# Small loads on spaced partitions in the last two passes, and the final pass without a loop

## The chip, the cores and the metric

The kernel runs on one core of a Trainium2 chip. The metric is the device time of one execution in microseconds (us). The times before are 3980.14, 3980.3 and 4032.01 us, the median 3980.3.

## The reference, cut to what matters

The input x has 16 images of 64 channels and 256 x 256 points, in float32. Two residual layers follow each other.

```
# layer 0
g   = groupnorm(x, groups=32)
F   = rfft2(g)[..., :32, :17]                       # 32 x 17 modes are kept
Y   = einsum('bhixy,hioxy->bhoxy', F, weight)       # 4 heads of 16 channels
x1  = x + irfft2(Y, padded with zeros) + bias
# layer 1, on g1 = groupnorm(x1, groups=32), all points of all images
m     = mean(g1);  mu = m / sqrt(m0^2 - |m1..|^2)   # Lorentz mean
alpha = max(g1_0 mu_0 - g1_rest . mu_rest, 1 + eps) # one value a point
d     = arccosh(alpha);  var = mean(d^2)            # over everything
v     = d / sqrt(alpha^2 - 1) * (g1 - alpha mu)
vo    = v - v_0 / (1 + mu_0) * (mu + e_0)
s     = gamma * vo_rest / (sqrt(var) + eps) + beta
out   = x1 + concat(sqrt(1 + |s|^2), s)             # channel 0, channels 1..63
```

## The kernel before, in words

Three passes read x. The first (`stage_a`) computes the kept modes and the norms' sums and writes the mixed modes to `spec`. It is not touched, apart from being followed by the others.

The middle pass (`stage_b`, from line 559) computes alpha and its relatives for every point of an image. x comes in eight tiles of 2 MB an image (`b_xt`, SyncE's queue, four buffers) and TensorE contracts the channels of each tile (L663). For the part of x1 that comes from the modes, GpSimd loads the image's modes into `b_spt` (`load_modes`, L753; 64 partitions, two loads of 32 rows each), VectorE contracts the channels in `combine` (products L818 and L824 with `arow` and `lrow`, sums L821 and L825, on 64 partitions x 2176 elements), and TensorE transforms the result (L673 to L685) and adds it to the contraction of x. `dense` (L839 to L868) then makes, from the finished image, the factor rows, splits each in three bf16 parts, and GpSimd stores them as `maps` (L773), `bmap` (L774) and `dmap` (L775), and only then takes up the next image: its weights (L747) and its `load_modes`. VectorE's order in a turn is combine of an image, then dense of the one before. GpSimd's order is weights, modes of the image, three words a channel into `spec` (L760), channel 0 of x (L767, after dense has read the last one), and the stores.

The final pass (`stage_c`, from line 967) writes the output. An image is 16 tiles of 128 partitions x 2048 (1 MB): partition p holds half a channel. Per tile TensorE makes the modes' part (L1118, from `c_mv`, whose last two rows of each half are loaded from bmap) and VectorE adds it to x (L1262); TensorE makes a factor and a shift (L1132, from `c_rt`: twelve rows, six to each half, as bf16, times a weight matrix `lwc` that is zero on all rows but those), VectorE multiplies (L1272), ScalarE copies the shift (L1198) and squares (L1205), GpSimd adds (L1323), TensorE sums the squares for channel 0 (L1143). Channel 0 is finished once an image and stored by itself (L1057, four stores of 32 rows).

SyncE issues every transfer of this pass, in a written order: per tile the small loads of the tile after next (per half three of `c_rt` with 6, 4 and 2 rows, L1032, and one of `c_mv`, L1033, so eight), the x load of that tile (L1022), the store of the tile two back (L1039). Once an image come channel 0's stores (L1057), two halves of modes for the next image (L1043) and `c_dmap` (L1049). The weights' rows of `c_rt` are marked in the constant `misc` (columns 12 to 23), which `place` (in the middle pass) turns into `keep["lw"]`. Images 1 to 14 are a hardware loop on each engine; as an operand can't be indexed by image in it, ScalarE copies that image's weights and two columns to `lwc` and `cols` (L1214, L1221) at its end.

Of the kernel before, what the change touches and what calls it, by code (L numbers as in the profile page):

```python
# [20 lines left out]
ALU = mybir.AluOpType  # L21
# [12 lines left out]
EPS = 1e-5  # L34


def constants():
# [521 lines left out]
def stage_b(nc, ctx, io, B, keep):  # L559
# [19 lines left out]
    NC_IN = 16 * 16  # L579

    with ExitStack() as mem:
# [13 lines left out]
        arow, lrow = sb("arow", [128, B, C]), sb("lrow", [128, B, C])  # L595
        aw, awc = sb("aw", [128, B, 2, 2]), sb("awc", [128, 2, 47])
# [4 lines left out]
        spt = sb("spt", [64, C, YS])  # L601
        prod = sb("prod", [64, C, M2])
# [15 lines left out]
        def _(sp):  # L618
# [16 lines left out]
            sp.dma_start(idft_h[0:64], cst["idft_d"]).then_inc(c_in, 16)  # L635
# [105 lines left out]
        def _(pool):  # L741
# [66 lines left out]
        def _(dve):  # L808
# [5 lines left out]
            def combine(b):  # L814

                dve.wait_ge(sp_in, b * 32 + 32)
# [5 lines left out]
                V.tensor_copy(vm[0:64, 1], spt[:, 0, 0:M2]).then_inc(v_ready, 1)  # L822
                dve.wait_ge(v_ready, b * 3 + 2)
                ch.step(V.tensor_tensor(prod[:], spt[:, :, 0:M2], over_m(lrow[0:64, b]), ALU.mult))  # L824
                V.tensor_reduce(vm[0:64, 2], prod[:].rearrange("p c m -> p m c"), AX_X, ALU.add).then_inc(v_ready, 1)  # L825
# [67 lines left out]
            ch.inc(V.memset(vm[:], 0.0))  # L893
            V.memset(idft_h[64:128], 0.0).then_inc(setup, 1)
# [72 lines left out]
def stage_c(nc, ctx, io, B, keep):  # L967
# [23 lines left out]
    with ExitStack() as mem:  # L991
# [23 lines left out]
        def _(sp):  # L1015
# [35 lines left out]
            def store_channel_0(b):  # L1051
# [4 lines left out]
                for j in range(4):  # L1056
                    sp.dma_start(o0_v[b, 0, j], o0[32 * j:32 * j + 32]).then_inc(o0_out, 16)  # L1057
# [342 lines left out]
```

## Time and profile before

| | |
|---|---|
| Runs, us | 3980.14, 3980.3, 4032.01 |
| Profiled execution, us | 4024.94, of which its span is 4023.4 |
| Granted TensorE clock, mean | 0.878 of full |
| Busy: PE, DVE, ACT, POOL | 75%, 68%, 53%, 38% |
| Transfers | 1199.08 MB, 298 GB/s over the span |
| SyncE's queue | 266126 packets, 1152.07 MB, 79.9% of 16 engines |

The profile is of one execution; a row's time is from the span's start. The first pass ends near 1130 us, the middle one near 2060 us, and the final one runs to the end. "Share" of the transfers is the mean busy share of the sixteen transfer engines (DMA engines). "To landing" is the time from a transfer's issue to its last completion. A queue's instructions carry the suffix q (SPq is SyncE's, POOLq GpSimd's).

### The profile page before, as it was taken

Reading aid. Unit: us, or ns where it says so; the run is one execution under the profiler, and the core shown is the slowest. Engines: PE = TensorE matmul, PEld = TensorE weight load, DVE = VectorE, ACT = ScalarE, POOL = GpSimd, SP = SyncE. Lnnn points to the kernel's source line nnn. Section 1 sums busy time; section 2 is a strip of 40 time slices with the busy share of each in tenths; the row PEclk is TensorE's granted clock in tenths of the full one; section 3 lists DMA queues with packets and bytes.
Section 4 is the critical chain, followed back from the end, with each engine's and each line's share of the span. In section 5 each row is a group of like instructions: output and inputs, shape, how many; then the busy total and the mean of one; then the engine's idle time right before and its main releaser. Section 6 shows DMA issues by size and latency. Waiting matters only on the chain. (4 is left out here: it accounts for less than half of the span.)

```text
span 4023.4 us, 77883 instructions
## 1 busy us (share of the span) xinstructions
PE 3002.5 (75%) x26018; PEld 1495.1 (37%) x26018; DVE 2748.0 (68%) x2969; ACT 2141.8 (53%) x2940; POOL 1513.6 (38%) x876
## 2 busy tenths in 40 slices
PE   6988898989446767677715877877777778877776
PEld 3555555555211222222203434344333344443332
DVE  1888888888865355555444767677777677777766
ACT  6777676767200011111014767677776677776665
POOL 0110101010111111111113766666666666666666
PEclk9988888988668888888857999999999999999999
DMA  9878777677269999999915989899999899999898
GB/s 373 287 256 282 260 265 274 244 285 253 76 259 354 325 341 376 362 361 374 334 53 183 337 313 329 313 325 321 313 315 320 306 330 334 329 334 311 311 314 288
DMA packets 280512, 1199.08 MB, mean 298 GB/s; under 512 B 35145, under 2 KB 37038, under 8 KB 197934
## 3 DMA queue, kind: packets, MB, share of 16 engines
q1 hardware_dynamic: 266126, 1152.07, 79.9%
q0 software_dynamic: 14112, 43.37, 3.4%
q8 instruction: 171, 2.80, 0.3%
q14 instruction: 103, 0.84, 0.1%
HBM read 883.53 MB, written 311.73 MB: 297 GB/s over the span
## 5 line engine op out<-in xcount | busy, mean ns | idle before, releaser
L1323 POOL TENSOR_TENSOR c_ot<-c_ot,c_pp 128x1024 f32<-128x1024 f32 x512 | 1211.8, 2368 | 727.0 <-DVE c_ot L1272 651.8
L1262 DVE SCALAR_TENSOR_TENSOR c_xt<-c_xt,keep_k,c_p_u 128x1024 f32<-128x1024 f32 x512 | 654.0, 1277 | 332.5 <-DMA c_xt<-in_x 170.8
L1118 PE MATMUL c_p_u<-c_mv,c_zc 64*128 64x256 f32 x4096 | 612.3, 420 | 225.1 <-DVE c_xt L1262 163.1
L1272 DVE SCALAR_TENSOR_TENSOR c_ot<-c_p_f,keep_k,c_xt 128x1024 f32<-128x1024 f32 x512 | 657.3, 1284 | 177.0 <-DMA out<-c_ot 134.4
L1198 ACT ACTIVATE c_pp<-c_p_p,c_cols 128x1024 f32<-128x1024 f32 x512 | 570.5, 1114 | 362.4 <-PE c_p_p L1132 359.0
L1205 ACT ACTIVATE c_sq<-c_xt,c_cols 128x1024 f32<-128x1024 f32 x512 | 584.2, 1141 | 139.5 <-DVE c_xt L1262 138.8
L1118 PEld LDWEIGHTS c_p_u<-c_mv,c_zc 64*128 64x128 f32 x4096 | 371.4, 195 | 532.9 <-DVE c_xt L1262 321.3
L327 ACT ACTIVATE a_junk<-a_xt 128x1024 bf16<-128x1024 f32 x512 | 537.2, 1053 | 28.8 <-DMA a_xt<-in_x 21.5
L246 PE MATMUL a_p_rows<-a_xt,a_dft_h 128*64 128x512 f32 x2048 | 517.5, 652 | 33.6 <-DMA a_bias_t<-in_bias 19.5
L1132 PE MATMUL c_p_f<-c_rt,c_lwc 64*128 64x512 bf16 x1024 | 328.0, 402 | 179.6 <-DVE c_ot L1272 161.3
L663 PE MATMUL b_p_al<-b_xt,b_awc 128*32 128x512 f32 x2048 | 312.4, 682 | 161.2 <-DMA b_xt<-in_x 116.3
L721 ACT ACTIVATE b_dn<-b_dn,b_minus 128x512 f32<-128x512 f32 x16 | 11.6, 722 | 730.4 <-DVE b_dn L842 730.4
L525 POOL TENSOR_TENSOR a_sm<-a_sm 128x8 f32<-128x8 f32 x16 | 26.7, 1670 | 931.0 <-DVE a_sm L460 931.0
L1132 PE MATMUL c_p_p<-c_rt,c_lwc 64*128 64x512 bf16 x1024 | 330.7, 405 | 0.0
L399 DVE TENSOR_REDUCE a_y<-a_prod 128x34 f32<-128x1088 f32 x256 | 317.4, 1281 | 5.7
L394 DVE TENSOR_TENSOR a_prod<-a_wm,a_xh 128x1088 f32<-128x1088 f32 x256 | 318.0, 1284 | 0.3
L818 DVE TENSOR_TENSOR b_prod<-b_spt,b_arow 64x2176 f32<-64x2176 f32 x16 | 38.7, 2417 | 393.3 <-DMA b_spt<-spec 393.3
L1143 PE MATMUL c_p_t<-c_sq,c_hw 128*32 128x512 f32 x2048 | 305.1, 671 | 1.2 <-ACT c_sq L1205 1.2
L663 PE MATMUL b_p_ls<-b_xt,b_awc 128*32 128x512 f32 x2048 | 297.3, 650 | 0.0
L1104 PEld LDWEIGHTS c_p_z<-c_idft,c_ys 128*37 128x37 f32 x7936 | 238.0, 116 | 111.3 <-issue 111.3
L1104 PE MATMUL c_p_z<-c_idft,c_ys 128*37 128x64 f32 x7936 | 277.3, 224 | 0.0
L271 PE MATMUL a_p_cols<-a_dft_w,a_cols 128*128 128x34 f32 x2048 | 264.5, 288 | 3.1 <-DVE a_xm L388 3.1
(209 smaller groups left out, 3029.8 us busy)
## 6 DMA issues: line engine op xcount, KB each, us to landing
a_xt<-in_x SPq DMA_DIRECT2D x256, 1024.0 KB, 8.0
b_xt<-in_x SPq DMA_DIRECT2D x128, 2048.0 KB, 16.0
c_xt<-in_x SPq DMA_DIRECT2D x256, 1024.0 KB, 16.7
out<-c_ot SPq DMA_DIRECT2D x256, 1024.0 KB, 18.4
maps<-b_maps POOLq DMA_DIRECT2D x64, 192.0 KB, 5.7
dmap<-b_dmap POOLq DMA_DIRECT2D x16, 768.0 KB, 11.6
c_rt<-maps SPq DMA_DIRECT2D x512, 24.0 KB
c_dmap<-dmap SPq DMA_DIRECT2D x16, 768.0 KB, 17.2
```

The lines of the kernel that those rows point to most:

```text
L246: last = nc.tensor.matmul(p_rows[i][64 * t:64 * t + 64, :], dft_h[:, j], xt[q % NX][:, t::2, i, j * W:(j + 1) * W], start=(j == 0), stop=( ...
L327: nc.scalar.activation(junk[h % 2][:].rearrange("p (i w) -> p i w", i=2), xt[q % NX][:, h], ACT.Square, accum_out=sq[:, q, h:h + 1]).then_ ...
L394: ch.inc(V.tensor_tensor(prod[o % 2][:], wm[:, o], xh[:].rearrange("p k n -> p (k n)").unsqueeze(1).to_broadcast((128, 2, CI * M2)), ALU.m ...
L663: last = nc.tensor.matmul(out[32 * j:32 * j + 32, :], awc[:, kind, 15 - k:47 - k], xt[t % NX][:, at:at + 512], start=(k == 0), stop=False, ...
L1104: last = nc.tensor.matmul(p_z[64 * at:64 * at + YS, 64 * c:64 * c + 64], ys[:, 8 * part + c], idft[:, chunk, at], start=True, stop=True)
L1118: last = nc.tensor.matmul(p_u[:, 512 * at + W * r:512 * at + W * r + W], zc[t // CH][64 * at:64 * at + 64, i], mv[t % NB][64 * at:64 * at ...
L1132: last = nc.tensor.matmul(p[:, 512 * k:512 * k + 512], lwc[at:at + 64], rt[t % NB][at:at + 64, c:c + 512], start=True, stop=True)
L1198: S.activation(pp[n][:], p_p[:], ACT.Identity, bias=cols[:, 1:2]).then_inc(pp_done, 1)
L1205: S.activation(sq[t % 2][:, 1024 * n:1024 * n + 1024], xt[t % NB][:, 1024 * n:1024 * n + 1024], ACT.Square, scale=cols[:, 0:1]).then_inc(s ...
L1262: V.scalar_tensor_tensor(out=u, in0=u, scalar=kc, in1=p_u[:], op0=ALU.mult, op1=ALU.add).then_inc(u_done, 1)
L1272: V.scalar_tensor_tensor(out=ot[t % NB][:, at], in0=p_f[:], scalar=kinv, in1=xt[t % NB][:, at], op0=ALU.add, op1=ALU.mult).then_inc(f_done, 1)
L1323: P.tensor_tensor(o, o, pp[n][:], ALU.add).then_inc(o_done, 1)
```

## The change

The loads of `c_rt` put their twelve rows at partitions 5, 15, ... 115, 14, 30, ... 126 and 16, 48, 80, 112 instead of 0 to 11 and 64 to 75, and both halves come with one load each: three loads a tile instead of six. The mask columns follow. The `c_ys` modes go to every second partition, with the constant `c_idft` beside them. Channel 0's four stores become one. In the middle pass `b_spt` holds two heads on each half of the partitions, so combine runs on 128 partitions x 1088 elements, with copies `ah` and `lh` of the factors; its load becomes four of 64 rows. The final pass is written out for all sixteen images, without the loop and without `lwc`, `cols` and `idle`.

```diff
+MAP_ROWS = ((5, 10), (14, 16), (16, 32))
...
-    for at, first in ((12, 0), (18, 64)):
-        for part, (row, rows) in enumerate(((0, 6), (6, 4), (10, 2))):
-            for s in range(2):
-                m[first + row + s:first + row + rows:2, at + 2 * part + s] = 1.0
+    for a, at in enumerate((12, 18)):
+        for part, ((first, step), rows) in enumerate(zip(MAP_ROWS, (6, 4, 2))):
+            for i in range(rows):
+                m[first + step * (rows * a + i), at + 2 * part + i % 2] = 1.0
...
-                for k in range(2):
-                    pool.dma_start(spt[KX * k:KX * k + KX].rearrange("k (h i) m -> k h (i m)", h=HEADS),
-                                   spec[b, k].rearrange("(h k) n -> k h n", h=HEADS)).then_inc(sp_in, 16)
+                for h in range(HEADS):
+                    half, i = 64 * (h // 2), 16 * (h % 2)
+                    pool.dma_start(spt[half:half + 64, i:i + 16].rearrange("p i m -> p (i m)"),
+                                   spec[b, :, KX * h:KX * h + KX]).then_inc(sp_in, 16)
...
-                over_m = lambda a: a.unsqueeze(2).to_broadcast((64, C, M2))
-                ch.step(V.tensor_tensor(prod[:], spt[:, :, 0:M2], over_m(arow[0:64, b]), ALU.mult))
+                over_m = lambda a: a.unsqueeze(2).to_broadcast((128, C // 2, M2))
+                ch.step(V.tensor_tensor(prod[:], spt[:, :, 0:M2], over_m(ah[:, b]), ALU.mult))
...
-                V.tensor_reduce(vm[0:64, 0], prod[:].rearrange("p c m -> p m c"), AX_X, ALU.add).then_inc(v_ready, 1)
+                V.tensor_reduce(vm[:, 0], prod[:].rearrange("p c m -> p m c"), AX_X, ALU.add).then_inc(v_ready, 1)
...
+            for half in range(2):
+                p, c = slice(64 * half, 64 * half + 64), slice(32 * half, 32 * half + 32)
+                ch.inc(V.tensor_copy(ah[p], arow[p, :, c]))
+                ch.inc(V.tensor_copy(lh[p], lrow[p, :, c]))
...
-    maps_v = io["maps"].rearrange("b m s (t n) -> b t (m s) n", n=TC)
+    maps_v = io["maps"].rearrange("b (a m) s (t n) -> b t a (m s) n", a=2, n=TC)
...
+                for (first, step), rows in zip(MAP_ROWS, (6, 4, 2)):
+                    sp.dma_start(r[first:first + step * (2 * rows - 1) + 1:step], maps_v[b, t, :, :rows]).then_inc(r_in[t % NB], 16)
                 for at in range(2):
-                    for row, rows in ((0, 6), (6, 4), (10, 2)):
-                        sp.dma_start(r[64 * at + row:64 * at + row + rows], maps_v[b, t, 6 * at:6 * at + rows]).then_inc(r_in[t % NB], 16)
                     sp.dma_start(m[64 * at + M2:64 * at + M2 + 2].rearrange("p (n r) -> p n r", n=2), bmap_v[b, t, at]).then_inc(r_in[t % NB], 16)
...
-                    sp.dma_start(ys[KX * k:KX * k + KX, 32 * half:32 * half + 32].rearrange("k (h i) m -> k h (i m)", h=2),
+                    sp.dma_start(ys[64 * k:64 * k + 64:2, 32 * half:32 * half + 32].rearrange("k (h i) m -> k h (i m)", h=2),
...
-                for j in range(4):
-                    sp.dma_start(o0_v[b, 0, j], o0[32 * j:32 * j + 32]).then_inc(o0_out, 16)
+                sp.dma_start(o0_v[b, 0], o0[:]).then_inc(o0_out, 16)
...
-            entry(0)
-            with sp.Fori(1, B - 1) as b:
-                entry(b)
-            entry(B - 1, last=True)
+            for b in range(B):
+                entry(b, last=b == B - 1)
...
-                S.activation(pp[n][:], p_p[:], ACT.Identity, bias=cols[:, 1:2]).then_inc(pp_done, 1)
+                S.activation(pp[n][:], p_p[:], ACT.Identity, bias=keep["cols"][:, b, 1:2]).then_inc(pp_done, 1)
```

The same replacement of the loop stands on the other four engines, and L1132 reads `keep["lw"]` of its image instead of `lwc`.

## Rows read from the trace of the kernel before

**Rows 1.** Windows, middle and final pass: us; busy (count) by engine; clock; DMA share; GB/s.
```profile
1260.00:1980.00 720.00, 499.94 (x3498) 165.00 (x3490) 357.60 (x325) 78.22 (x117) 116.70 (x218) 0.84 0.94 350
2205.20:3949.50 1744.30, 1364.00 (x15402) 690.54 (x15404) 1279.05 (x1022) 1230.18 (x1293) 1157.45 (x497) 0.94 0.92 321
```

**Rows 2.** The line L1049 (once an image): duration in ns min/median/max, first and last start.
```profile
L1049 SPq DMA_DIRECT2D c_dmap<-dmap x16: 332/392/970, 2205.2 to 3949.5; - x16
```

**Rows 3.** SyncE's order of time, first tiles of the final pass: start us, us, instruction.
```profile
2188.27 0.37 SPq L1039 DMA_DIRECT2D out<-c_ot  x1
...
2199.29 0.37 SPq L1039 DMA_DIRECT2D out<-c_ot  x1
```

**Rows 4.** Transfers from 2100 to 2129 us, while c_mv's 37 constant rows load.
```profile
DMA packets 637, 0.65 MB, mean 22 GB/s; under 512 B 5, under 2 KB 637, under 8 KB 637
...
q1 hardware_dynamic: 637, 0.65, 6.7%
```

**Rows 5.** SyncE's order of time at the loop's back edge in the final pass.
```profile
3074.60 0.38 SPq L1039 DMA_DIRECT2D out<-c_ot  x1
3081.72 1.05 SPq L1032 DMA_DIRECT2D c_rt<-maps  x3
```

**Rows 6.** Windows before and after that back edge reaches the transfers.
```profile
3076.00:3081.00 5.00, 4.07 (x56) 2.35 (x54) 3.90 (x4) 3.77 (x5) 3.50 (x3) 1.00 0.97 298
3082.40:3086.40 4.00, 1.37 (x8) 1.08 (x10) 0.61 (x1) 1.40 (x4) 2.83 (x2) 0.88 0.19 70
```

**Rows 7.** Transfers of one image, 3019.6 to 3139.3 us: GB/s in 40 slices, packets.
```profile
GB/s 264 331 414 372 426 349 379 297 382 282 311 375 407 231 256 348 374 374 168 259 360 68 211 315 368 305 412 374 295 258 339 312 315 329 320 391 128 242 287 285
DMA packets 6266, 37.44 MB, mean 313 GB/s; under 512 B 1108, under 2 KB 1108, under 8 KB 2132
```

**Rows 8.** Order of time in the middle pass: one turn, then the first and last loads.
```profile
1543.49 0.56 POOL L775 DMA_DIRECT2D dmap<-b_dmap  x1
1544.70 1.22 POOL L753 DMA_DIRECT2D b_spt<-spec  x2 [0.45 <-issue]
1561.16 2.42 DVE L818 TENSOR_TENSOR b_prod<-b_spt,b_arow 64x2176 f32<-64x2176 f32 x1 [25.46 <-DMA b_spt<-spec]
1563.62 4.22 DVE L821 TENSOR_REDUCE b_vm<-b_prod 64x34 f32<-64x2176 f32 x1
...
1575.28 0.75 DVE L839 TENSOR_SCALAR b_dn<-b_p_al,b_ac 128x512 f32<-128x512 f32 x1 [0.59 <-DVE b_vm L825]
...
1590.57 0.59 POOL L773 DMA_DIRECT2D maps<-b_maps  x1 [10.96 <-DVE b_maps L868]
...
1596.72 1.22 POOL L753 DMA_DIRECT2D b_spt<-spec  x2 [0.44 <-issue]
...
1252.65 1.20 POOL L753 DMA_DIRECT2D b_spt<-spec  x2 [0.16 <-issue]
...
1980.52 1.23 POOL L753 DMA_DIRECT2D b_spt<-spec  x2 [0.44 <-issue]
```

**Rows 9.** The page's transfers: out<-in, queue, count, KB each, median us to landing.
```profile
c_xt<-in_x SPq DMA_DIRECT2D x256, 1024.0 KB, 16.7
...
c_rt<-maps SPq DMA_DIRECT2D x512, 24.0 KB
c_dmap<-dmap SPq DMA_DIRECT2D x16, 768.0 KB, 17.2
b_spt<-spec POOLq DMA_DIRECT2D x32, 296.0 KB, 16.1
...
c_mv<-bmap SPq DMA_DIRECT2D x512, 8.0 KB
```

**Rows 10.** Groups by line, final pass: a table load of ScalarE at each turn's head.
```profile
L1198 ACT ACT_TABLE_LOAD x14 | 18.0, 1283 | 43.4 <-PE c_p_p L1132 43.3
```

**Rows 11.** The page's groups: VectorE on 128x1088, in the first pass.
```profile
L399 DVE TENSOR_REDUCE a_y<-a_prod 128x34 f32<-128x1088 f32 x256 | 317.4, 1281 | 5.7
L394 DVE TENSOR_TENSOR a_prod<-a_wm,a_xh 128x1088 f32<-128x1088 f32 x256 | 318.0, 1284 | 0.3
```

More of the change, by code:

```diff
@@ L634, in _ @@
             sp.dma_start(btrow[:], row(io["beta"], C)).then_inc(c_in, 16)
-            sp.dma_start(idft_h[0:64], cst["idft_d"]).then_inc(c_in, 16)
+            for half in range(2):
+                sp.dma_start(idft_h[64 * half:64 * half + 64], cst["idft_d"]).then_inc(c_in, 16)
             sp.dma_start(idft_w[:], cst["idft_w"]).then_inc(c_in, 16)
@@ L923, in _ @@
             ch.step(V.tensor_tensor(v1[:], over_b(brow[:]), srow[:, :, 1], ALU.subtract))
+            for half in range(2):
+                p, c = slice(64 * half, 64 * half + 64), slice(32 * half, 32 * half + 32)
+                ch.inc(V.tensor_copy(ah[p], arow[p, :, c]))
+                ch.inc(V.tensor_copy(lh[p], lrow[p, :, c]))
             ch.inc(V.tensor_scalar(q2[:], srow[:, :, 0, 0], s1(5), None, ALU.mult))
@@ L1001, in stage_c @@
         sq = [sb(f"sq{k}", [128, TC]) for k in range(2)]
-        lwc = sb("lwc", [128, 2 * C], BF16)
-        cols, idle = sb("cols", [128, 2]), sb("idle", [128, 1])
         dmap = sb("dmap", [128, 3, 512])
@@ L1123, in factors @@
                 g = b * GR + 2 * t + n
-                if t == 0 and n == 0:
-                    pe.wait_ge(w_ready, b + 1)
                 if not (is_at(b, 0) and t == 0 and n == 0):
@@ L1131, in factors @@
                         c = 1024 * n + 512 * k
-                        last = nc.tensor.matmul(p[:, 512 * k:512 * k + 512], lwc[at:at + 64], rt[t % NB][at:at + 64, c:c + 512], start=True, stop=True)
+                        last = nc.tensor.matmul(p[:, 512 * k:512 * k + 512], keep["lw"][at:at + 64, b].rearrange("p c s -> p (c s)"), rt[t % NB][at:at + 64, c:c + 512], start=True, stop=True)
                 last.then_inc(f_mm, 1)
@@ L1164, in _ @@
             pe.wait_ge(c_in, 16 * (2 + 2 * NB))
-            pe.wait_ge(filled, 3)
+            pe.wait_ge(filled, 2)
             for part in range(8):
@@ L1174, in _ @@
                 ins.then_inc(z_mm, 1)
-            entry(0)
-            with pe.Fori(1, B - 1) as b:
-                entry(b)
-            entry(B - 1, last=True)
+            for b in range(B):
+                entry(b, last=b == B - 1)
             sums(B - 1, T - 1)
@@ L1211, in root @@
                 S.activation(th[:], arg[:], ACT.Sqrt).then_inc(th_ready, 1)
-            def weights(b):
-                S.activation(lwc[:], keep["lw"][:, b].rearrange("p c s -> p (c s)"), ACT.Copy).then_inc(w_ready, 1)
-            def columns(b):
-                if not is_at(b, 0):
-                    act.wait_ge(pp_done, b * GR)
-                    act.wait_ge(sq_done, b * GR)
-                    S.activation(idle[:], idle[:], ACT.Copy).then_inc(cols_free, 1)
-                S.activation(cols[:], keep["cols"][:, b], ACT.Copy).then_inc(cols_ready, 1)
             def entry(b, last=False):
@@ L1229, in entry @@
                     shift(b, t, 1)
-                    if t == T - 1 and not last:
-                        weights(b + 1)
                     square(b, t, 1)
@@ L1234, in entry @@
                         root(b - 1)
-                if not last:
-                    columns(b + 1)
-            weights(0)
-            columns(0)
             act.wait_ge(zeroed, 2 * NB + 2)
-            act.wait_ge(filled, 3)
+            act.wait_ge(filled, 2)
             for part in range(8):
                 copy_part(0, part, part + 1)
-            entry(0)
-            with act.Fori(1, B - 1) as b:
-                entry(b)
-            entry(B - 1, last=True)
+            for b in range(B):
+                entry(b, last=b == B - 1)
             root(B - 1)
@@ L1298, in _ @@
             V.memset(ys[:], 0.0).then_inc(zeroed, 1)
-            V.memset(idft[64:128], 0.0).then_inc(filled, 1)
+            V.memset(idft[:], 0.0).then_inc(zeroed, 1)
             V.memset(p_z[:], 0.0).then_inc(filled, 1)
-            V.memset(idle[:], 0.0).then_inc(zeroed, 1)
             V.memset(hw[:], 0.0).then_inc(chain, 1)
@@ L1306, in _ @@
             ch.done = 1
-            entry(0)
-            with dve.Fori(1, B) as b:
-                ch.loop(b, 1, PER_C)
+            for b in range(B):
                 entry(b)
-                ch.end(B - 1)
             channel_0(B - 1)
@@ L1336, in entry @@
                         channel_0(b - 1)
-            entry(0)
-            with pool.Fori(1, B) as b:
+            for b in range(B):
                 entry(b)
             channel_0(B - 1)
-PER_C = 2
 def program(nc, args, B):
```

35 lines of the change are left out of this document (16 added, 19 removed).

## The prediction

> **What bounds the kernel now.** I read the page's slices and queues first, then the two later passes (from lines 559 and 967) in windows, then the packets of single stretches, then SyncE's and VectorE's order of time. The profiled execution took 4024.9 us, 1.1% over the median of the runs, 3980.3; all differences below are worked out against the profiled one and put on the median. The change leaves the first pass (to about 1130 us) alone.
>
> The final pass, from 2205 to 3950 us, has the transfer engines busy for 0.92 of the time at 321 GB/s, while no compute engine passes 0.8 [rows 1]. An image takes (3949.5 - 2205.2)/15 = 116.3 us, 7.27 us a tile [rows 2]. Compute alone can do 5.51 us: that is the step of the first tiles (11.02 us for two), before SyncE's queue has filled [rows 3]. So transfers set the pace. But which? Two rows show that it isn't all sixteen engines. A load onto 37 rows runs at 22 GB/s and 6.7% of the engines, one of sixteen [rows 4]: a load goes to as many engines as its rows divide into. And at the loop's back edge SyncE issues nothing for 6.7 us [rows 5]; the engine share then falls from 0.97 to 0.19 [rows 6], three engines' worth, with 70 GB/s still moving. Some engines hold a backlog that the others don't. Who they are follows from a count: in one image 1108 packets are under 512 B [rows 7], where no data row is that small; they are completions, one for each engine that took part. The 41 wide transfers of an image (32 of x and out, 4 of modes, 1 of dmap, 4 of channel 0) take 656. The other 452, 28 a tile, are the eight small loads: 2 x (6 + 4 + 2 + 2). Each small load therefore uses as many engines as its outermost count, and I take them to be the same first ones each time. Per tile the first two engines then carry 6 rows of 4 KB of c_rt and 8 KB of c_mv beside their 128 KB of x and out.
>
> A check: a busy engine moves 321/(0.92 x 16) = 21.8 GB/s. Per image the first two have 2.10 MB of x and out (33.5 MB over sixteen), 0.52 MB small and 0.10 MB of the rest (c_dmap, c_ys, channel 0; sizes in [rows 9]): 125 us at that rate, against 116 measured; the others have 101 us. The first two must run 7% better (23.4 GB/s) while others idle, which fits. They are the bound, and the rest has 13% slack.
>
> The middle pass is different: 56.0 us an image ((1980.5 - 1252.7)/13), in a closed circle that one turn shows [rows 8]: POOL issues b_spt at 1544.7; it lands at 1561.2; combine takes VectorE to 1575.0; dense and its casts last until POOL can store the maps at 1590.6; after the nine stores it issues the next b_spt at 1596.7: 52.0 us with no slack in it.
>
> **The change, part by part.**
>
> *Final pass, c_rt (L1032).* Six loads a tile become three, of 12, 8 and 4 rows; with c_mv five issues where there were eight. SyncE's issues of 0.3 us each [rows 5] are saved, 0.9 us a tile, hidden: its stretched issues are back pressure, it is ahead of the data (c_xt lands 16.7 us after its issue [rows 9]). The bytes stay. What counts is rows on the first two engines, now 6. Bounds: if each load's rows spread one to an engine, 3 rows, -3 x 0.175 us x 16 = -8.4 us an image (-134 us in all; 4096 B at 23.4 GB/s is 0.175 us); if all three went to two engines, 12 rows, +16.8 us (+269). The source of the 12 is evenly spaced (six of six rows), so it is one count of 12. The sources of the 8 and of the 4 are two separate groups, 2 x 4 and 2 x 2; the nearest row is c_mv, a 2 x 2 pattern of four pieces, which by the count above uses 2 engines, not 4. So I take 1 + 4 + 2 = 7 rows: +1 row, +2.8 us an image, 45 us in all.
> The Trainium skill ("DMA: Bandwidth & Descriptors", section "Why a DMA increments its semaphore by 16 and not by 1") says that the engine count is the largest up to 16 that divides the slowest dimension of both sides, and on SyncE's queue the lowest-numbered engines. It names 12, 2 and 2 engines for the new loads; the trace's 28 completions agree with it, and no row here shows a load whose two sides differ in this.
>
> *Channel 0's store (L1057).* Four stores of 32 rows become one whose outermost count is 4: by the same reading 32 rows of 2 KB on each of four engines instead of 8 on all: +49 KB on the first two, 2.1 us an image, 34 us in all. Bounds 0 (if it spreads) to 34.
>
> *Landing places.* The small rows now land from partition 5 to 126 instead of 0 to 11 and 64 to 75. What that relieves no row shows; from below nothing, from above the whole lag of the first two, 15 us an image. The check above closes without any crowding, so I take a value near the lower end, a tenth: 1.6 us an image, -25 us.
>
> *No loop.* The back edge costs SyncE some 6 us more than its usual gap [rows 5] and ScalarE a table load of 1.28 us at its head [rows 10]. I cost it at nothing: the two late engines work through it on their backlog (rows 6's 70 GB/s). If that cover were gone, it would be up to the 4 us lull a turn, 56 us. Copies of lwc and cols (ScalarE) go as well; ScalarE is not the bound.
>
> *Middle pass, combine (L818 to L825).* Two products of 64x2176 at 2.42 us and two sums at 4.22 us become 128x1088. The product of that size takes 1.28 us [rows 11]; a sum is half of 4.22, 2.1 (the contiguous one of the same size takes 1.28 [rows 11], this one is strided). 13.9 us become 7.3: -6.6 a turn, between -8.3 and -5.
>
> *Middle pass, load of the modes (L753).* Two loads of 32 rows become four of 64 rows, the source in two groups of 32. By the same reading each goes to 2 engines. Whether the four pairs differ no row shows; the ends are one pair for all and four pairs, and I take four, which is nearer to the even load that every transfer from this queue shows now: 76 KB on each of eight engines instead of 38 on all. Per engine dmap's 48 KB and b_spt's 38 KB land in 17.7 us (1543.5 to 1561.2), beside the x stream: 4.9 GB/s. So +38 KB are +7.7 us. Bounds: 0 if they still use sixteen; +54 us if all four went to the same two (303 KB each). Landing is in the circle, and POOL issues two more (0.6 us each) but behind dmap's packets: nothing. Net +1.1 us x 14 turns = +15 us. If the circle gets shorter, the x stream, at 350 GB/s now [rows 1], has room for it: slices of the final pass reach 426 [rows 7].
> The same page says that loads from GpSimd take their two engines in turn, by a cursor, which gives eight and +7.7 us; no run here shows it yet.
>
> *One-offs.* Four copies (ah, lh) and one more constant load ahead of the first turn, about 2 us; three store issues less at the very end, -1.
>
> Sum: +45 + 34 - 25 + 0 + 15 + 1 = +70 us: 4095 on the profiled execution, **4050** on the median (+1.8%).
>
> **Rivals.**
> 1. *Relief.* The small rows sat on the same few partitions that the first engines write x to; spread, both run freely. For it: the two late engines are just those. Against: the rate check closes without it. If half of the 15 us lag goes, -7.6 us x 16 = -122, and with the middle pass level 3860. The Trainium skill ("SBUF — State Buffer", "Door 1: The DMA port swizzle") holds that partitions 0 to 63 reach only half of the ports to the memory and four adjacent ones a single port; by that rule the time falls, by some part of this sum. No row here separates one port's load from another's.
> 2. *Only the middle pass gains.* b_spt still lands in 16 us: -6.6 x 14 = -92, the final pass +54: 3942.
> 3. *Slower.* The twelve rows go to two engines as well (their source is written as two halves): 12 rows instead of 7, +5 x 0.175 x 16 x 16 = +224 on the forecast: 4275. It decides as soon as the first load's completions are 2 instead of 12. The fixed pair in the middle pass would be worse still (+46 x 14 = +640 and more).
> 4. *It does nothing*: the 321 GB/s are the memory's own limit for reads mixed with writes, and the lull is mere order. Against: slices of the same image reach 426 GB/s [rows 7]. 3980.
>
> **Chances.** Forecast 0.46, its own range 4010 to 4110, of which 0.2 lies over 4060 (2%, about what a measurement of this kernel can tell from no change); relief 0.20, most of it below 3900; middle pass only 0.12; slower 0.13; nothing 0.09. Faster by over 2%: 0.18. Slower by over 2%: 0.20 + 0.13, with a little of the tails 0.34. Within: 0.48. A range from 3860 to 4130 leaves out the slower rival, the deeper half of the relief at most, and little else, about 0.2 together.
>
> **What would show it.** Completions per image: the small loads should leave 12 + 2 + 2 + 4 = 20 a tile instead of 28, channel 0 leaves 4 instead of 64, so the packets under 512 B fall from 1108 to 37 x 16 + 4 + 320 = 916. If there are 28 a tile or more, the loads spread and I am wrong on them. The final pass's image should take 119 to 121 us with its busy share lower than 0.92; a share that rises means relief. In the middle pass combine's rows should read 1.28 and 2.1 us and b_spt's landing about 24 us. The forecast is wrong if the landing stays at 16, or if the final pass falls under 114 us an image; a fall of just some 4 us at the images' borders would say that the back edge did cost.

## The result and the profile after

The changed kernel takes **4284.6 us** (median of 4 runs, 4248.6 to 4294.0), the kernel before 3994.8 us in its runs beside it: ratio 1.069, 95% interval 1.060 to 1.078. Some executions of these kernels are over 1.5% slower than the fastest of the same kernel; ratios and intervals here are of the others, which leaves out one run of e11 at 4574 us. The forecast was 4050 us, 1.8% slower, with a range up to 4130; it is 7% slower. The rival with the same size (4275) is not what happened either, as the packets will show. The profiled execution took 4248.6 us (span 4247.0) against 4024.9 (4023.4) before: +223.6 us.

Where they lie: first the two later passes in windows, as [rows 1] for the kernel before (us; busy and count of PE, PEld, DVE, ACT, POOL; clock; share of the transfer engines; GB/s).

```profile
1295.50:2229.40 933.90, 518.25 (x3566) 165.63 (x3570) 275.01 (x325) 78.23 (x117) 138.50 (x248) 0.77 0.76 271
2455.00:4171.60 1716.60, 1366.34 (x15416) 691.28 (x15412) 1274.45 (x1023) 1189.46 (x1221) 1157.33 (x497) 0.94 0.90 326
```

The first window goes from the third image's load of the modes to the last's, the second from the first to the last load of dmap; here are the issues that bound them.

```profile
1295.54 2.02 POOL L757 DMA_DIRECT2D b_spt<-spec  x3
2229.35 2.04 POOL L757 DMA_DIRECT2D b_spt<-spec  x3 [0.43 <-issue]
L1053 SPq DMA_DIRECT2D c_dmap<-dmap x16: 417/425/906, 2455.0 to 4171.6; - x16
```

**Middle pass:** (2229.35 - 1295.54)/13 = 71.8 us a turn, 56.0 before [rows 8]: 13 x 15.8 = +206 us, with the share of the transfer engines down from 0.94 to 0.76. The turns ahead of this window add 43 us (1295.5 against 1252.65). **Final pass:** (4171.6 - 2455.0)/15 = 114.4 us an image, 116.3 before [rows 2]: -28 us. 206 + 43 - 28 is 221 of the 223.6 us. So the pass that I had put at +15 us lost 249, and the one that I had put at +54 gained 28.

One turn of the middle pass after, in order of time (start us, us, instruction, idle before and who ended it); [rows 8] is its like.

```profile
1658.83 1.38 POOL L757 DMA_DIRECT2D b_spt<-spec  x2 [0.43 <-issue]
1661.44 1.31 POOL L757 DMA_DIRECT2D b_spt<-spec  x2 [1.22 <-issue]
...
1665.02 56.23 SPq L645 DMA_DIRECT2D b_xt<-in_x  x8
...
1698.00 1.29 DVE L822 TENSOR_TENSOR b_prod<-b_spt,b_ah 128x1088 f32<-128x1088 f32 x1 [46.01 <-DMA b_spt<-spec]
1699.33 2.17 DVE L825 TENSOR_REDUCE b_vm<-b_prod 128x34 f32<-128x1088 f32 x1
...
1705.63 0.75 DVE L843 TENSOR_SCALAR b_dn<-b_p_al,b_ac 128x512 f32<-128x512 f32 x1 [0.43 <-DVE b_vm L829]
...
1719.50 0.69 DVE L872 TENSOR_TENSOR b_maps<-b_dn,b_maps 128x512 bf16<-128x512 f32 x1
1720.91 0.59 POOL L777 DMA_DIRECT2D maps<-b_maps  x1 [10.93 <-DVE b_maps L872]
...
1727.03 1.36 POOL L757 DMA_DIRECT2D b_spt<-spec  x2 [0.43 <-issue]
```

The circle is the forecast's, with combine at its forecast price (1.29 and 2.17 us; 1698.0 to 1705.6 instead of 1561.2 to 1575.3). What grew is the first step: 39.2 us from the first issue of b_spt to the product, 16.5 in the turn of [rows 8]. Over all 16 images the page says it by VectorE's wait and GpSimd's queue, first before, then after (line, instruction, count | busy us, mean ns | idle us before it and who ended it; queue: packets, MB, share).

```profile
q0 software_dynamic: 14112, 43.37, 3.4%
...
L818 DVE TENSOR_TENSOR b_prod<-b_spt,b_arow 64x2176 f32<-64x2176 f32 x16 | 38.7, 2417 | 393.3 <-DMA b_spt<-spec 393.3
```

```profile
q0 software_dynamic: 28960, 43.48, 3.6%
...
L822 DVE TENSOR_TENSOR b_prod<-b_spt,b_ah 128x1088 f32<-128x1088 f32 x16 | 20.7, 1293 | 755.6 <-DMA b_spt<-spec 755.6
```

The wait grew by 362 us; less 16 x 6.6 for the shorter combine that is +257, the 249 above. And the queue carries the same 43.4 MB in twice the packets: 14848 more, 928 an image, worth 0.11 MB: 896 of 8 bytes and 32 completions of 4, as the trace's packet sizes say. Nobody wrote these packets in the kernel. Two stretches of the turn above show what they do (packets, MB; then by queue): 1663 to 1667 us, and 1684 to 1697 us.

```profile
DMA packets 924, 0.90 MB, mean 224 GB/s; under 512 B 776, under 2 KB 778, under 8 KB 918
...
q0 software_dynamic: 918, 0.80, 79.7%
q1 hardware_dynamic: 6, 0.10, 14.8%
```

```profile
DMA packets 402, 5.52 MB, mean 425 GB/s; under 512 B 65, under 2 KB 65, under 8 KB 65
...
q1 hardware_dynamic: 379, 5.52, 99.9%
q0 software_dynamic: 23, 0.00, 0.1%
```

While the x loads pause, 918 packets pass in 4 us, most of the tiny ones among them. SyncE resumes x at 1665.0, and from then on the rest drips: 23 packets in 13 us, together 0.00 MB. In the same 13 us x moves 5.52 MB, 337 packets of 16 KB, 21 on each of sixteen engines. 23 against 21: as if one engine gave its turns alternately to a packet of x and to a tiny packet of b_spt. Taken one by one, these 23 (22 of 8 bytes, one of 4) follow each other at steps of 0.62 us, but for two that share a step with a neighbour; and 425 GB/s over sixteen engines is 26.6 GB/s, at which 16 KB take 0.62 us.

The data of b_spt, 128 packets of 4736 bytes an image, are all there by 1672 us in this turn; VectorE waits for a few last tiny packets. Over the 16 turns the last of the 8-byte packets starts 0.7 to 1.7 us before the product every time, while the last data packet ends 0.6 to 28 us before it: the data take turns as well and are sometimes as late. Which engine carries the last packets the trace doesn't say. How many carry the data it does say roughly: from 1667 to 1668 us only data packets of b_spt run in GpSimd's queue, and they take 0.54 of sixteen engines, about four pairs.

```profile
q0 software_dynamic: 25, 0.12, 53.6%
```

For the final pass, the transfers of its 15 images, before and after.

```profile
DMA packets 93628, 559.85 MB, mean 321 GB/s; under 512 B 16562, under 2 KB 16562, under 8 KB 31799
```

```profile
DMA packets 90685, 558.83 MB, mean 326 GB/s; under 512 B 13737, under 2 KB 13737, under 8 KB 28948
```

13737/15 = 915.8 completions an image against 916 forecast (16562/15 = 1104 before): the loads of 12, 8 and 4 rows use 12, 2 and 2 engines, and channel 0's store four.

### The profile page after: what moved, and what is told of

It is laid out like the page before. It is cut to its first block and busy times, and to the rows that moved or that the text cites. A ratio compares the mean times of both kernels' runs of the same rounds, so it can differ in the third digit from the quotient of the medians.

```text
span 4247.0 us, 70119 instructions
## 1 busy us (share of the span) xinstructions
PE 3008.1 (71%) x26018; PEld 1487.6 (35%) x26018; DVE 2641.7 (62%) x2971; ACT 2099.4 (49%) x2866; POOL 1538.7 (36%) x908
## 3 DMA queue, kind: packets, MB, share of 16 engines
q0 software_dynamic: 28960, 43.48, 3.6%
## 5 line engine op out<-in xcount | busy, mean ns | idle before, releaser
L1296 POOL TENSOR_TENSOR c_ot<-c_ot,c_pp 128x1024 f32<-128x1024 f32 x512 | 1212.0, 2368 | 688.5 <-DVE c_ot L1249 687.3
L1193 ACT ACTIVATE c_pp<-c_p_p,keep_cols 128x1024 f32<-128x1024 f32 x512 | 570.7, 1115 | 453.8 <-PE c_p_p L1131 453.4
L1119 PE MATMUL c_p_u<-c_mv,c_zc 64*128 64x256 f32 x4096 | 618.6, 423 | 173.5 <-DVE c_xt L1239 116.8
L1200 ACT ACTIVATE c_sq<-c_xt,keep_cols 128x1024 f32<-128x1024 f32 x512 | 583.3, 1139 | 105.5 <-DVE c_xt L1239 105.0
L822 DVE TENSOR_TENSOR b_prod<-b_spt,b_ah 128x1088 f32<-128x1088 f32 x16 | 20.7, 1293 | 755.6 <-DMA b_spt<-spec 755.6
L1131 PE MATMUL c_p_f<-c_rt,keep_lw 64*128 64x512 bf16 x1024 | 327.0, 401 | 200.1 <-DVE c_ot L1249 195.7
L1131 PE MATMUL c_p_p<-c_rt,keep_lw 64*128 64x512 bf16 x1024 | 329.7, 404 | 0.0
L771 POOL DMA_DIRECT2D b_dn<-in_x x64 | 32.9, 518 | 727.1 <-DVE b_dmap L844 723.8
## 6 DMA issues: line engine op xcount, KB each, us to landing
out<-c_ot SPq DMA_DIRECT2D x256, 1024.0 KB, 19.5
```

The costliest lines, as they stand in the source:

```text
L1119: last = nc.tensor.matmul(p_u[:, 512 * at + W * r:512 * at + W * r + W], zc[t // CH][64 * at:64 * at + 64, i], mv[t % NB][64 * at:64 * at ...
L1131: last = nc.tensor.matmul(p[:, 512 * k:512 * k + 512], keep["lw"][at:at + 64, b].rearrange("p c s -> p (c s)"), rt[t % NB][at:at + 64, c:c ...
L1193: S.activation(pp[n][:], p_p[:], ACT.Identity, bias=keep["cols"][:, b, 1:2]).then_inc(pp_done, 1)
L1200: S.activation(sq[t % 2][:, 1024 * n:1024 * n + 1024], xt[t % NB][:, 1024 * n:1024 * n + 1024], ACT.Square, scale=keep["cols"][:, b, 0:1]) ...
L1296: P.tensor_tensor(o, o, pp[n][:], ALU.add).then_inc(o_done, 1)
```

## The experiments

All ratios are to the kernel before, with their 95% interval; "a turn" and "an image" are worked out as above, each from that kernel's trace. "From issue to VectorE's start" in the expectations is the mean over the 14 turns from the third image on: 20.2 us before, 42.2 after.

**One pass of the change at a time.** The middle pass of the kernel before under the changed final pass (e1), and then the changed combine with its modes loaded evenly (e2):

```
-  for h in range(HEADS):                      # four loads, two engines each
-      ... dma_start(spt[half:half+64, i:i+16], spec[b, :, KX*h:KX*h+KX])
+  for half in range(2):                       # e2: four loads, sixteen engines each
+      for k in range(2): at = 64*half + KX*k
+          ... dma_start(spt[at:at+KX] as "k (h i) m", h=2,
+                        spec[b, k] as "h k n" -> "k h n" [:, 2*half:2*half+2])
```

> The changed kernel with the middle pass put back as it was (combine on 64 partitions, two loads of 32 rows); the final pass as changed. Theory A (the whole loss is in the middle pass's load of the modes): the middle pass's turn goes back to 56 us, the final pass keeps its 114.4 us an image, so the time is 25 to 35 us under the kernel before: ratio 0.992. Rival B (the final pass with its seven rows on the first engines lost it): ratio 1.03 or more.

> The changed kernel, with combine on 128 partitions kept, but b_spt loaded by four loads of 32 rows whose outermost count is 32 on both sides, so each goes to all sixteen engines. Theory A: q0's packets fall back from 28960 to about 14100, b_spt's landing (issue of the first to VectorE's start) from 39 us to 16, combine stays at 7.3 us, so a turn takes 52 to 50 us instead of 71.8 and the whole is 4285 - 14 x 21 = about 3990 - 28 - 80 = 3880, ratio 0.97. Rival C (combine's new layout itself costs, by its reading of 128 partitions or the copies ah and lh): the turn stays over 60 us, ratio over 1.02.

e1: 0.998 (0.994 to 1.002), an image 114.5 us, a turn 56.7: the loss is the middle pass's alone, though the gain is less than the 25 to 35 us expected. e2: 0.989 (0.982 to 0.996), 3952.7 us, a turn 52.7: with the same combine, the same bytes and as many loads as in the change, 332 us less than the change. So it is the shape of b_spt's four loads and nothing else. (The time taken by GpSimd to issue them isn't it: 64 issues take 34.7 us in all in e2 and 42.9 in the change, half a microsecond an image.) The expected 3880 us was missed. The turn is 4 us shorter than e1's and not 6.6, since now the transfers fill it, which the middle pass in windows shows: share 1.00, against 0.92 in e1.

```profile
1247.00:1931.90 684.90, 505.39 (x3566) 163.78 (x3565) 275.31 (x325) 78.23 (x117) 132.38 (x248) 0.87 1.00 375
```

```profile
1248.00:1984.90 736.90, 507.56 (x3566) 166.84 (x3570) 357.57 (x325) 78.26 (x117) 119.11 (x222) 0.84 0.92 349
```

**How many loads are narrow.** e2's kernel with one (e5) and with two (e6) of the four heads loaded as the change does it.

```
+  for h in range(1):  # e6: range(2)
+      ... the change's two-engine load of head h; the other heads by even loads
```

> The kernel of e2_even_modes with one of an image's b_spt loads as the changed kernel has it (64 rows on two engines), the other three heads in three loads on many engines. Theory of the turns: a two-engine load from GpSimd's queue also puts as many tiny packets on every other engine as it has packets on its pair, and each waits its turn between x packets; the delay grows with the number of such loads. From first issue to VectorE's start it was 23.2 us with none (e2) and 42.2 us with four: about 28 us with one, turn of the middle pass about 56 to 58 us, time 3952 + 14 x 4 = about 4010 us. Rival, the bytes on two engines: the pair's 300 KB come as late whether one, two or four pairs are loaded, so nearly all of the delay stands already with one: 38 to 42 us, turn about 70 us, time about 4200 us.

> As e5_one_narrow, with two of the four heads loaded on two engines each. Theory of the turns: about 33 us from issue to start, turn about 61 to 64 us, time about 4080 to 4120 us, that is about half of the way from e2 (3953) to the changed kernel (4285). Rival, the bytes on two engines: the same as with one, about 70 us a turn.

e5: 1.011 (1.007 to 1.014), 4046 us, a turn 58.7. e6: 1.031 (1.027 to 1.035), 4125 us, a turn 62.7. Beside e2's 52.7 and the change's 71.8 that is 6.0, 10.0 and 19.1 us for one, two and four. The rows of the page of e2, e5 and e6:

```profile
q0 software_dynamic: 14624, 43.37, 3.3%
...
L823 DVE TENSOR_TENSOR b_prod<-b_spt,b_ah 128x1088 f32<-128x1088 f32 x16 | 20.7, 1292 | 447.0 <-DMA b_spt<-spec 447.0
```

```profile
q0 software_dynamic: 18464, 43.40, 3.5%
...
L829 DVE TENSOR_TENSOR b_prod<-b_spt,b_ah 128x1088 f32<-128x1088 f32 x16 | 20.7, 1292 | 531.2 <-DMA b_spt<-spec 531.2
```

```profile
q0 software_dynamic: 21792, 43.43, 3.5%
...
L826 DVE TENSOR_TENSOR b_prod<-b_spt,b_ah 128x1088 f32<-128x1088 f32 x16 | 20.7, 1292 | 613.3 <-DMA b_spt<-spec 613.3
```

The change's 28960 packets and 755.6 us stand above. Packets an image above e2: 240, 448, 896; wait an image above e2: 5.3, 10.4, 19.3 us. Each narrow load adds 224 packets of 8 bytes, as many as 16 on each of the fourteen engines that carry none of its data, and about 5 us. (e5 has five loads instead of four; the fifth's 16 completions make the 240.) The delay falls on whatever stands behind in the queue: in e5 and e6 the last data packet ends 0.8 to 1.7 us before the product in every turn, and the last 8-byte packet has started long before, 8.3 to 19.5 us in e5 and 4.6 to 6.6 in all but one turn of e6. There VectorE waits for the data of the even loads that were issued behind the narrow ones. The forecast's picture (a pair of engines has 38 KB more each) would have cost the same with one pair as with four; it falls.

**The packet behind which they wait.** The changed kernel with the middle pass's x in two halves of 8 KB a row (e13), and four small two-engine loads beside the even ones of the kernel before (e9):

```
-  sp.dma_start(xt[...][:], x_v[b, t])                       # e13
+  for k in range(2): sp.dma_start(xt[...][:, 2048*k:2048*k+2048], x_v[b, t][:, 2048*k:...])
+  for j in range(4):                                        # e9, ahead of b_spt's two loads
+      pool.dma_start(extra[...64 rows, j], spec[b, :, KX*j:KX*j+KX, 0:16])
```

> The changed kernel, with the middle pass's x loaded in two halves of 8 KB a row instead of one load of 16 KB a row; b_spt still by four two-engine loads. Theory of the turns (each 8-byte packet of b_spt waits for one x packet on its engine): half the packet, about half the wait, so of the 19 us that b_spt lands later than with even loads about 9 stay: 42.2 becomes about 32 us, a turn about 62 us, time about 4285 - 14 x 10 = 4145 us. Rival, the bytes on two engines or an x stream that takes the engines as a whole: the wait doesn't hang on the packet's size, 42 us, 71.8 a turn, 4285 us.

> The kernel before, its two b_spt loads as they were, and ahead of them four more loads an image from GpSimd's queue of the changed kernel's shape (64 rows in two groups, so two engines each), but with only 64 bytes a row, 16 KB in all, into a buffer that nobody uses; VectorE waits for them too. Theory of the turns: the time goes with the number of packets that wait their turn between x packets, not with bytes: from first issue to VectorE's start +15 to +25 us against 20.2, a turn of the middle pass about 70 us, time about 4200 us. Rival, the bytes on two engines: 16 KB are under 1 us, and four issues more 2.4 us: turn 57 to 59 us, time 4010 to 4040 us.

e13: 1.025 (1.020 to 1.031), 4103 us, a turn 64.0, issue to start 35.1 us; 181 us faster than the change with not one packet less in GpSimd's queue:

```profile
q0 software_dynamic: 28960, 43.48, 3.7%
...
L823 DVE TENSOR_TENSOR b_prod<-b_spt,b_ah 128x1088 f32<-128x1088 f32 x16 | 20.7, 1292 | 626.9 <-DMA b_spt<-spec 626.9
```

The wait above e2's is 11.2 us an image instead of 19.3. Half the packet gave 0.58 of the wait: the delay hangs on the size of x's packets, as turns do and bytes don't.

e9 gave 1.011 (1.007 to 1.015), 4058 us, a turn 59.5: not the 70 us of my theory, nearly the rival's. The page says why it did not test it:

```profile
q0 software_dynamic: 16160, 43.75, 3.6%
...
L821 DVE TENSOR_TENSOR b_prod<-b_spt,b_arow 64x2176 f32<-64x2176 f32 x16 | 38.7, 2418 | 443.4 <-DMA b_spt<-spec 443.4
```

2048 packets more, 32 a load: one or two on each engine, since rows this short go many to a packet (data packets of 2048 bytes, others of 128). So a two-engine shape alone is cheap (3.1 us an image of waiting for four such loads); it is dear when its data make many packets. I had taken the shape for the count.

**The parts of the final pass, one by one,** each alone on the kernel before.

```
e3:  for b in range(B): entry(b, last=b == B-1)     # written out, copies lwc and cols stay
e4:  c_rt by the change's loads of 12, 8 and 4 rows at its places
e7:  sp.dma_start(o0_v[b, 0], o0[:])                # one store of channel 0
e8:  ys[64*k:64*k+64:2, ...], idft[0:128:2]         # modes on every second partition
e14: e3 with keep["lw"], keep["cols"] read in place, copies and their waits gone
e10: ys[64+KX*k:64+KX*k+KX, ...], idft[64:128]      # modes on the upper half, no gaps
```

> The kernel before, with only the final pass's loop written out for 16 images (lwc, cols and all loads as they were). My forecast's view (the two late engines cover the back edge): an image stays at 116.3 us, ratio 1.000. Rival: the back edge's lull of 4 us an image was real loss: 112 to 114 us an image, ratio 0.985 to 0.992.

> The kernel before, loop and all, with only the c_rt loads changed (12, 8 and 4 rows at spaced partitions, three loads instead of six). By the count of rows on the first engines (6 to 7): 119 us an image, ratio 1.01. By relief at the landing places: under 115 us an image, ratio 0.99 or less.

> The kernel before with channel 0 stored by one transfer an image instead of four, and nothing else. The prediction's step: +2.1 us an image, about 116.3 + 2.1 = 118.4 us, time about 4030 us. Rival, from e1_final_pass_only (114.5 us an image though rows cost 1.7 and the written-out loop 0.6): this part is what gains about 4 us, an image of 112 to 113 us, time about 3935 us. If neither, 116 to 117 us and 3996 us, the gain is another part's or only the parts' together.

> The kernel before with the final pass's modes (c_ys) and their inverse matrix on every second partition, and nothing else. The prediction gave this part -1.6 us an image (other engines carry the rows): 114.7 us an image, time about 3970 us. Rival, from the parts that cost so far: it carries the whole missing gain of about 4 us, 112 to 113 us an image and 3935 us. If neither: 116 to 117 us and 3996 us.

> e3_no_loop (loops written out, +18 us by ratio) without the copies lwc and cols that ScalarE makes at each image's end and without their waits, as in the changed kernel; everything else as in the kernel before. The prediction cost the copies at nothing: then 1.0046 x 3996 = 4014 us. Rival, from the sum of the parts (rows +36, loop +18, store +17, modes' place -41 make +30, the whole final pass measured -9): the copies' removal is the missing -39 us: about 3975 us.

> The kernel before with the final pass's modes (c_ys) and their inverse matrix on partitions 64 to 127 instead of 0 to 63, without gaps, and nothing else; e8_modes_step had them on every second partition and ran at 0.990 of the kernel before. If the spread over the partitions is what gains, this one gives 3996 us, the kernel before's. If it is only that the lower partitions are left free, this one gives 3968 us as well, or less.

| part, alone | forecast, us | ratio (95%) | as us of 3996 | an image in its trace, us |
|---|---|---|---|---|
| e4, rows | +45 | 1.009 (1.005 to 1.013) | +36 | 117.9 |
| e3, loop written out | 0 | 1.005 (1.001 to 1.008) | +18 | 116.8 |
| e14, the same without copies | 0 | 1.006 (1.002 to 1.009) | +22 | 117.2 |
| e7, one store | +34 | 1.004 (1.001 to 1.007) | +17 | 115.7 |
| e8, modes' places | in the -25 | 0.990 (0.986 to 0.993) | -41 | 112.8 |
| e10, modes on the upper half | | 0.994 (0.990 to 0.998) | -24 | 112.8 |
| e1, the whole final pass | +54 | 0.998 (0.994 to 1.002) | -9 | 114.5 |

(An image of the kernel before is 116.3 us in its trace, but that execution lies 29 us above its median; so the ratios decide, and a difference of an image or less than 1.5 us says little.) For single parts every sign of the forecast is right but one: the written-out loop costs a little instead of nothing. For the whole final pass the sign is wrong, +54 against -9. The copies to `lwc` and `cols` cost nothing that e3 and e14 could tell apart. (They are in the kernel before although a loop there does index operands by image, as ScalarE's copy in L1214 and VectorE's product in L818 do; no run here shows a limit of that kind.) The relief is larger than forecast and lies in a place that I had not named: the modes, not the small rows. e10 has the images of e8 without any gaps between the rows, and the intervals of the two overlap. So the spread isn't needed; it is enough that the modes leave the first 64 partitions, or half of them do. What they cross there, a port or the other writes to those rows, is open.

**Do the parts add?** e17 has rows and modes' places together, e18 the whole final pass but with four stores.

```
e17: e4 + e8
e18: e1 with  for j in range(4): sp.dma_start(o0_v[b, 0, j], o0[32*j:32*j+32])
```

> The kernel before with two parts of the change together: c_rt in three loads at the new places (alone, e4: +36 us) and the final pass's modes on every second partition (alone, e8: -41 us); loop, copies and four stores stay. If parts add: -5 us, about 3990 us. Rival, from e1 (whole final pass -9 where the parts sum to about +34): the two take away the same waits or help each other, and together they give about -45 us: 3950 us, with loop and store costing their +18 and +17 on top.

> e1_final_pass_only (the changed final pass, the middle pass as before: -9 us) with channel 0 stored in four stores again. It stands between e17_rows_and_step (+22 us) and e1: with the loop written out and the copies gone, but not the one store. If the single store costs here what it cost alone (+17 us), this one is 17 us faster than e1, about 3970 us, and the written-out loop with the copies gone is worth -48 us beside the new rows, against +22 alone. Rival: the store is what gains beside the new rows, and this one is at about 4000 to 4020 us, no faster than e17.

e17: 1.006 (1.003 to 1.008), +22 us, where the sum is -5 and the rival had -45. e18: 0.994 (0.990 to 0.997), -26 us, so the one store costs 17 us here as it did alone, and the written-out loop without copies is worth 48 us beside the new rows (+22 to -26) though alone it cost 22. The parts sum to +34 and give -9. Nor do rows and modes' places add: beside the new rows the places are worth 14 us (+36 to +22) and not 41. The next experiments show one side of this.

**Fewer rows on the first engines.** Even modes with the modes' step and the rows of before (e11); then c_rt with 5 rows on the first two engines, by another order of the 8-row load (e12) and by splitting it (e15); e16 is e15's rows in the changed kernel.

```
e11: e2's middle pass + e8
e12: e11 + c_rt by three loads, the 8-row load's source as "q a n" instead of "a q n"
e15: e11 + c_rt by loads of 12, 4, 4, 4 rows (the 8 rows split by a)
e16: the change + even modes + four stores + e15's loads; loop written out, no copies
```

> The two parts that gained, and nothing else of the change: the middle pass of e2_even_modes (combine over 128 partitions, modes by four loads on sixteen engines) and the modes of the final pass on every second partition. If the gains add: 3968 - 31 (e1 to e2) = 3937 us, turn 52.7 us, image 112.8 us. If the faster middle pass only moves the wait: 3968 us.

> e11_even_and_step with c_rt in three loads at the changed kernel's places, the load of 8 rows in such an order that its outermost count is 8 instead of 2: 8 engines with one row each, so the first two carry 1 + 1 + 2 = 4 rows of c_rt, against 6 in the kernel before and 7 in the changed one. The prediction's step (2.8 us a row on the first engines): 2 rows less, -5.6 us an image, about 3937 - 90 = 3850 us. Rival: rows on the first engines don't set the pace, and what the loads cost (e4: +36 us) is their number or their landing places: 3937 to 3975 us.

> e11_even_and_step with c_rt at the changed kernel's places by loads of 12, 4, 4 and 4 rows (the load of 8 rows split by its two groups), so the first two engines carry 1 + 2 + 2 = 5 rows a tile against 6 before and 7 in the change; 22 completions a tile. By the prediction's 2.8 us a row: an image 2.8 us shorter than e11's 113.2, about 110.4 us, time about 3942 - 45 = 3897 us. Rival: the rows on the first engines don't set the pace: 3942 us or more.

> The changed kernel with three things mended: b_spt by four even loads, the load of 8 rows split in two of 4 (first two engines 5 rows instead of 7), and channel 0 in four stores again. From e2's 3953 us: two rows less at the prediction's 2.8 us each make -5.6 us an image, four stores -1 us an image: 3953 - 90 - 17 = about 3845 us. Rival, if a row is worth only half of that: about 3890 us.

e12's order puts rows of either half where the other half's matmuls read them, so its factors are of other data; its transfers and instructions are as many. It had 1007 completions an image, 22 a tile: the 8 rows went to four engines, two each, not to eight as expected, so the first two carried 1 + 2 + 2 = 5. e15's transfers (15 images) give 16076/15 = 1072, 26 a tile, 12 + 4 + 4 + 2 with c_mv's four; 22 in its expectation was a miscount. Its first two engines carry 1 + 1 + 1 + 2 = 5 too.

```profile
L1059 SPq DMA_DIRECT2D c_dmap<-dmap x16: 332/338/457, 2150.9 to 3793.7; - x16
...
DMA packets 93133, 559.84 MB, mean 341 GB/s; under 512 B 16076, under 2 KB 16076, under 8 KB 31301
```

e11: 0.981 (0.970 to 0.992), 3936 us, as the sum of its parts. e12: 0.969 (0.960 to 0.977), 110.6 us an image, 2.6 less than e11's 113.2. e15: **0.970 (0.965 to 0.975), 3879 us**, an image 109.5. One row less on the first two engines is -2.6 and -3.7 us an image, forecast 2.8; by ratio 47 and 41 us, with e11's wide interval. e11 has the rows at their old places and in six loads. e12 and e17 have the same places, three loads each and the same loop, so their final passes differ in the rows alone: 116.3 us an image with seven rows, 110.6 with five, 2.8 a row. e12 itself was expected at 3850 us with four rows and gave 3890 with five.

e16, with the written-out loop, is slower than e15: 0.979 (0.975 to 0.983), 3913 us, an image 112.1. Its expectation was 3845 us, and 3890 if a row were worth only half; it lies above both. The reason shows beside e18, the same final pass with seven rows: 113.5 us an image, so two rows less give 1.4 us there and not 5.7. By ratio, seven rows to five, with the even middle pass coming in both times, is -0.035 with the loop (e17 to e15) and -0.015 without it (e18 to e16). The written-out loop takes away most of what the rows cost: it is worth -48 us beside seven rows, costs 18 to 22 with the old six and 34 with five (e15 to e16). How it does that no run shows.

The version to keep is e15: 3% faster than the kernel before and 9% than the change. Both its passes in windows; the final pass moves 341 GB/s at share 0.95, against 321 at 0.92 [rows 1]:

```profile
1248.20:1935.70 687.50, 503.49 (x3566) 162.00 (x3570) 275.30 (x325) 78.24 (x117) 132.40 (x247) 0.87 1.00 375
2151.00:3793.70 1642.70, 1338.42 (x15416) 681.31 (x15412) 1280.70 (x1022) 1227.96 (x1292) 1158.64 (x497) 0.96 0.95 341
```

## Why the prediction was wrong

**The step that failed is the load of the modes in the middle pass.** It said: each load goes to 2 engines, the four pairs differ, 38 KB more on each of eight engines at 4.9 GB/s, +7.7 us. The first two statements agree with the runs (32 data packets a load, and 0.54 of the engines busy with them). The third took bytes for the whole cost. Measured is +22.6 us an image of waiting ((755.6 - 393.3)/16): each load also puts 224 tiny packets in the queue, and they and the data packets behind them each wait a turn behind a 16 KB packet of x. (22.6 - 7.7) x 16 = +238 us; the forecast of 4095 on the profiled execution was 154 too low, since the final pass was 82 us better than forecast (-28 against +54).

The value lay inside my bounds for that term (0 to +54 a turn), but I put no rival on it between 7.7 and 54, called it worse than the slower rival and left it out of the range. The fallacy was in the sentence "nearer to the even load that every transfer from this queue shows now": no two-engine load from GpSimd's queue was in the trace, so nothing bounded its landing but the 54, and it sits in a circle without slack, 16 times.

The rule of the Trainium skill ("DMA: Bandwidth & Descriptors", "Why a DMA increments its semaphore by 16 and not by 1") agrees with the runs: 916 completions on SyncE's queue, and about four pairs at work for four loads on GpSimd's. The same section says that a load from that queue is completed by all 16 engines whatever its shape. I had read it for the number of pairs and not for what the others must do. And the page's "Queues, rings and completion order" says that an engine goes round its queues packet by packet; the 23 packets against 21 of x and e13's halved packets agree. Had I put the two together with x's 16 KB packets, a slower rival of this mechanism would have stood there. That each narrow load adds packets beyond its data, 224 of 8 bytes, only e5, e6 and the change show.

**What was right.** The circle of the middle pass, and combine's price: 1.29 and 2.17 us against 1.28 and 2.1. The engines of every small load, to the completion. The first engines as the bound of the final pass, as long as it keeps its loop: one row more costs 36 us alone (forecast 45), two less 5.7 us an image (forecast 5.6, e17 to e12). In the written-out form, which is the change's own, a row is worth about a quarter of that (e18 to e16), so +45 was too much there. The single store's sign, at half its size (17 of 34).

**What was right by luck or not at all.** "No loop: nothing" is +18 to +22 alone and -48 beside the new rows. "Landing places: a tenth of the lag, -25" is -41 and belongs to c_ys; the relief rival, which said the small rows, is not it: they moved in e4, and that kernel got slower. The rival "only the middle pass gains" has it the wrong way round.

**The slower rival** named a time near the result (4275) by another mechanism, twelve rows on two engines; completions of 916 exclude it.

## What to carry to other kernels

In this kernel a load from GpSimd's queue that goes to two engines puts tiny packets beside its data, and it and the loads behind it are done only when these have passed between the packets of the other queue. So ahead of any reshaping of a load, count its engines; if it goes to few engines in many packets while large transfers run, expect its landing to grow with the packets on an engine and the time of the other queue's packet, not by bytes alone: here 5 us for each load of 224 additional packets beside packets of 16 KB. Where the same data can be cut by rows so that each load uses all engines (e2), that alone turned 4285 us into 3953. And where SyncE's small loads sit on the same first engines, count the rows on them, but measure the row in the form of the loop that is kept: a row was worth 2.8 us an image in one form and 0.7 in the other (one profiled execution each).

## What the runs showed of the hardware

- Two-engine loads of 148 KB on GpSimd's queue each put 224 additional packets of 8 bytes on the queue. They pass at over 190 in a microsecond while x pauses (776 packets under 512 B in 4 us), and the last ones at one in 0.62 us beside x packets of 16 KB.
- Rows of 64 bytes go many to a packet: a load of 64 such rows made 32 packets over all engines, completions included (e9), one of 64 rows of 2368 bytes 32 of data and 224 tiny ones beside its completions.
- On SyncE's queue no such packets appear: a two-engine load adds two completions (916 an image).
- TensorE's mean granted clock in the middle pass is lower where TensorE is busy for less of the time: 0.77 at a busy share of 0.55 (the change), 0.84 at 0.69 (before), 0.87 at 0.74 (e2). What that costs no run separates.
- The same modes landing on partitions 64 to 127, or on every second one, instead of 0 to 63, made the kernel 24 to 41 us faster, and 14 beside the new rows; not foreseen in this size, and its cause is open.
- The same two rows less on the first two engines took 5.7 us off an image with the final pass in a loop and 1.4 us with it written out; the cause is open.
